# Merged value bursts, another order of maximum tiles, and divisions moved up in the tail of a fused attention and feed-forward kernel

## The chip, the cores and the metric

The kernel runs on one core of a Trainium2 chip. The metric is the device time of one execution in microseconds. The engines are PE (TensorE), DVE (VectorE), ACT (ScalarE), POOL (GpSimd) and SP (SyncE, which here issues all the DMAs).

## What is computed

The input x has 1024 tokens of 256 numbers, in float32. The reference is one block of a network:

```
x = x + layernorm(attention(layernorm(x)))
x = x + layernorm(ffn(layernorm(x)))

attention(h): gates[0] * main(h) + gates[1] * pattern(h)
  main:    16 heads with low-rank q and kv (ranks 192 and 64), 128 + 64 wide
           (the 64 with rotary positions), softmax over 1024 keys, values of 128, o_w
  pattern: 16 heads of width 16, softmax over 1024 keys, sp_o_w
ffn(h): gelu(h @ dq(up_kernel) + up_bias) @ dq(down_kernel) + down_bias
  dq: each block of 32 along K is put on an FP4 grid with a power-of-two scale
```

## The kernel before

All five engines run programs written out by hand, in order, tied by semaphores. There are three parts: a prologue (transposes, first projections), the attention, and an epilogue (output projections, normalisations, the feed-forward part).

**The attention** goes through ten slots v = 0 to 9 of 16 steps s. In slot v (1 to 8) the scores of head pair v-1 are computed while the operands of pair v are prepared. PE makes tiles, each in one of three PSUM buffers `xb` of two banks, which are used strictly in turn. A tile can start when the buffer's last tile has been read. The tiles:

- T(s): a step's pattern scores, one pair of matmuls; ACT reads them with an exponential into `ep`.
- M(s): a step's main scores, seven pairs of matmuls; ACT reads them with an exponential into `em`.
- pm (16 a slot, one pair each) and mm (16 a slot, two pairs each): scores of a quarter of the queries, of which DVE takes the maximum (lines 1170 and 1178).
- P0 to P3: projections; DVE and ACT read them (`rc` is DVE's product with the cosines). sk, sv, oT, vo: tiles of slot 0 alone, in which DVE has a share for P and sk.
- S: sums of the accumulated exponentials, which ACT reads to `sums`.

`PM_STEP` says how many pm tiles each step has; from step 3 on the first comes between T and M, a second one behind M. Then come the step's mm tile, P and S. `FIRST` is the list of slot 0's tiles. At the end of a step PE runs the value matmuls, in which four 32-column parts of the array work side by side, one set of them a `main_values` (in `pvm`) for the step before, and in odd steps a `pattern_values` (in `pvp`) as well. POOL adds up `em`, and turns the rotary halves.

DVE also quantises the feed-forward weights in between: 4 chunks of 18 steps (`quantize`), some in the slots by `QPLAN`, two a step in slot 8, and the rest behind the attention (`last_quantized`). Each pair's sums go by DMA (`gather`) to `rs`, are inverted (`main_reciprocal`, `rec_done`), and go through DRAM to a broadcast copy (`spread`). DVE then divides (`main_division`). The pattern does the same with `prs` and `prec`. All this is queued on SP in order.

**The epilogue**: PE makes eight output projections o0 to o7 (line 1539 and 1541), where o0 to o3 need the first half of the contexts and o4 to o7 also the last main division, number 15, and the last pattern division, whose result SP moves to `wst`. On DVE `mix(t)` adds the scaled parts of projection t, `first_norm(t)` and `second_norm(t)` normalise (POOL computes the root between). PE transposes the results of tiles 0 to 3 (`xT`, line 1707), projects them up (line 1770), ACT applies gelu, PE projects down, and DVE normalises and adds.

Of the kernel before, what the change touches and what calls it, by code (L numbers as in the profile page):

```python
# [33 lines left out]
P = 128  # L34
# [8 lines left out]
NP = H // 2  # L43
# [391 lines left out]
ORDER = [0, 2, 3, 1]  # L435
UNIT_STEP = {0: 0, 2: 1, 3: 3, 1: 5}
UNIT_FIRST = {0: 0, 2: 1, 3: 4, 1: 7}
PM_STEP = [0, 0, 1, 1, 1, 1, 2, 2, 1, 2, 1, 2, 2, 0, 0, 0]
MM_LATE = 9
QSTEPS = 18  # L440


QPLAN = {1: {13: 1, 14: 1, 15: 2}, 2: {0: 1, 1: 1, 13: 1, 14: 1, 15: 2}, 3: {0: 1, 1: 2, 13: 1, 14: 1, 15: 2},
# [4 lines left out]
def quantized_at(v, s):  # L448

    return (1 if s < 3 else 2) if v == NP else QPLAN.get(v, {}).get(s, 0)  # L450
# [7 lines left out]
    [("pm", 5), ("P", 3), ("pm", 6), ("sv", 2)],  # L458
    [("pm", 7), ("sk", 3), ("pm", 8)],
    [("oT", 0), ("pm", 9), ("oT", 1)],  # L460
    [("P", 1), ("pm", 10), ("oT", 2)],
    [("sk", 4), ("mm", 0), ("mm", 1)],
    [("pm", 11), ("oT", 3), ("sv", 3)],
    [("mm", 2), ("oT", 4), ("pm", 12)],
    [("mm", 3), ("oT", 5), ("pm", 13)],
    [("mm", 4), ("oT", 6), ("pm", 14)],
    [("mm", 5), ("oT", 7), ("pm", 15)],
    [("mm", 6), ("oT", 8), ("mm", 7)],
    [("vo", 0), ("vo", 1), ("mm", 8), ("vo", 2), ("vo", 3)],
]  # L470
BY_ACT = ("S", "oT", "vo", "sv")
# [8 lines left out]
def x_steps(v):  # L480
# [4 lines left out]
    for s in range(16):  # L485
        step = []
        if v <= NP:
            step.append(("T", s))
        ahead = min(PM_STEP[s], 1) if s > 2 else 0
        if v < NP:  # L490
# [3 lines left out]
        if v < NP:  # L494
            step += [("pm", pm + i) for i in range(ahead, PM_STEP[s])]
            pm += PM_STEP[s]
        late = [MM_LATE + s] if v < NP else [MM_LATE + 2 * s, MM_LATE + 2 * s + 1]
# [14 lines left out]
def attention(nc, a, d, g, sem, done):  # L512
# [11 lines left out]
    with ExitStack() as ctx:  # L524
# [44 lines left out]
        oT = ep[:, :, :].rearrange("p a b -> p (a b)").rearrange("p (h n) -> p h n", n=HID)  # L569
# [70 lines left out]
        NSTACK = 12  # L640
        QUANTIZE, SIGN = QSTEPS + 2, 15
        NBACK = 4 + 1 + 4 * PDIRECT + DIRECT
# [495 lines left out]
        def vector_program(dve):  # L1138
# [160 lines left out]
            q_step = 0  # L1299
            for v in range(NP + 1):  # L1300
                for s in range(NS):
# [9 lines left out]
                    for _ in range(quantized_at(v, s)):  # L1311
                        if q_step < 4 * QSTEPS:
                            quantize(*divmod(q_step, QSTEPS))
                            q_step += 1

            def last_quantized(part):
                for step in (range(q_step, 4 * QSTEPS - 4) if part == 0 else range(max(q_step, 4 * QSTEPS - 4), 4 * QSTEPS)):
                    quantize(*divmod(step, QSTEPS))

            return {"main_reciprocal": main_reciprocal, "main_division": main_division, "last_quantized": last_quantized,  # L1320
                    "pattern_reciprocal": pattern_reciprocal, "pattern_division": pattern_division}

        def tensor_program(pe):
# [39 lines left out]
            def main_values(it, s):  # L1363
                q, kt = s // NT, s % NT
                if kt == 0 and (it or q):

                    pe.wait_ge(ctx_out, 2 * it + q)
                pe.wait_ge(em_ready, NS * it + s + 1)
                for h in range(2):
                    for r in (0, 32):  # L1370
                        mm = pe.matmul(pvm[64 * h + r:64 * h + r + 32, :], cpair[:, kt, 0, r:r + 32], em[:, 2 * s % 8 + h, :],  # L1371
                                       start=(kt == 0), stop=(kt == NT - 1))
                mm.then_inc(pvm_done, 1)

            def pattern_values(it, kt):
                if kt == 0:
                    pe.wait_ge(vp_in[it % 2], 16 * (it // 2 + 1))
                    if it:
                        pe.wait_ge(pat_out, it)
                pe.wait_ge(ep_ready, NS * it + 2 * kt + 2)  # L1380
                for hh in range(4):
                    mm = pe.matmul(pvp[32 * hh:32 * hh + 32, :], vp[:, it % 2, kt, hh, :], ep[:, (4 * kt + hh) % 8, :],  # L1382
                                   start=(kt == 0), stop=(kt == NT - 1))
                mm.then_inc(pvp_done, 1)
# [102 lines left out]
            for v in range(NP + 1):  # L1487
                for s in range(NS):
                    for tile in xs[v][s]:
                        x_tile(v, tile)  # L1490
                    if s == 0 and v >= 2:
                        main_values(v - 2, NS - 1)
                    if s and 1 <= v <= NP:
                        main_values(v - 1, s - 1)
                    if s == 1 and v >= 2:
                        pattern_values(v - 2, NT - 1)
                    if s >= 3 and s % 2 and 1 <= v <= NP:
                        pattern_values(v - 1, (s - 3) // 2)
# [14 lines left out]

    done |= {"scores_done": (x_ready, x_index[(NP + 1, "S", 1)] + 1), "bank_emptied": bank_emptied, "ctx_back": (ctx_back, 16 * NBACK), "ctx_ready": ctx_ready, "pat_back": pat_back}
    return sync_program, pool_program, tensor_program, scalar_program, vector_program


# [28 lines left out]
def epilogue(nc, a, d, g, sem, done, out):  # L1546
# [12 lines left out]
    with ExitStack() as ctx:  # L1559
# [64 lines left out]
        def evacuated(eng, n):  # L1624

            for s, kinds in ((ev_down, ("down",)), (ev_dve, ("o", "xT"))):
                count = sum(j[0] in kinds for j in jobs[:n + 1])
                if count:
                    eng.wait_ge(s, count)
            count = sum(ups[:n + 1])  # L1630
            if count:
                eng.wait_ge(gelu_out, count)
                last = [j for j in jobs[:n + 1] if j[0] == "up" and j[1:] in hi_by_act]
                eng.wait_ge(h_hi[0], len(last))
# [179 lines left out]
        def vector_program(dve, attention_rest):  # L1814
# [8 lines left out]
            def bn_stats(tiles, srcs):  # L1823
                for t, s in zip(tiles, srcs):
                    ins = dve.bn_stats(stats[:, t, :], s)  # L1825
                link(ins)

            def bn_aggregate(kind, tiles):
                for t in tiles:
                    ins = dve.bn_aggr(mv[:, kind, t, :], stats[:, t, :])  # L1830
                ins.then_inc(var_ready, 1)
# [7 lines left out]
            def mix(t):  # L1839

                n, y = index[("o", t)], ya[:, t % 4, :]
                dve.wait_ge(ya_scaled, t + 1)
                dve.scalar_tensor_tensor(y, bank[n % 8][:, 0:HID], gates[:, t, 0:1], y, ALU.mult, ALU.add).then_inc(ev_dve, 1)
                evacuated(dve, n)
                bn_stats([t], [y])
                bn_aggregate(0, [t])

            def first_norm(t):
                y, r = ya[:, t % 4, :], res[:, t, :]
                link(normalise(0, range(t, t + 1), [y], [y]))  # L1850
                if t == 0:
                    dve.wait_ge(res_in, 16)
                dve.tensor_tensor(r, r, y, ALU.add).then_inc(ya_added, 1)
                dve.wait_ge(ya_added, t + 1)
                bn_stats([t], [r])
                bn_aggregate(1, [t])

            def second_norm(t):
                normalise(1, range(t, t + 1), [x2[:, t, :]], [res[:, t, :]]).then_inc(x2_ready, 1)
# [41 lines left out]
            attention_rest["pattern_reciprocal"](NP - 1)  # L1901
            attention_rest["last_quantized"](1)
            attention_rest["main_reciprocal"](2 * NP - 1)
            mix(0)
            first_norm(0)
            mix(1)
            second_norm(0)
            attention_rest["pattern_division"](NP - 1)
            first_norm(1)
            mix(2)  # L1910
            second_norm(1)
            attention_rest["main_division"](2 * NP - 1)
            first_norm(2)
            for t in range(3, 6):
                mix(t)
# [161 lines left out]
```

## Time and profile before

| | us |
|---|---|
| Median of 3 runs (lowest, highest) | 790.09 (786.98, 792.28) |
| The profiled execution | 788.47 |
| Its span | 786.7 |
| PE busy | 751.6 (96% of the span) |
| DVE busy | 574.2 (73%) |
| POOL busy | 431.9 (55%) |
| ACT busy | 391.9 (50%) |

Matmuls are pipelined, so a busy PE is not PE at its peak. An idle time in brackets behind a row is counted from the modelled end of the matmuls before, which is later than the moment at which the next one could have started. The starts of the matmuls are therefore the better measure of what a wait costs.

### The profile page before, as it was taken

Reading aid. Unit: us, or ns where it says so; the run is one execution under the profiler, and the core shown is the slowest. Engines: PE = TensorE matmul, PEld = TensorE weight load, DVE = VectorE, ACT = ScalarE, POOL = GpSimd, SP = SyncE. Lnnn points to the kernel's source line nnn. Section 1 sums busy time; section 2 is a strip of 40 time slices with the busy share of each in tenths; the row PEclk is TensorE's granted clock in tenths of the full one; section 3 lists DMA queues with packets and bytes.
Section 4 is the critical chain, followed back from the end, with each engine's and each line's share of the span. In section 5 each row is a group of like instructions: output and inputs, shape, how many; then the busy total and the mean of one; then the engine's idle time right before and its main releaser. Section 6 shows DMA issues by size and latency. Waiting matters only on the chain. (4 is left out here: it accounts for less than half of the span.)

```text
span 786.7 us, 13921 instructions
## 1 busy us (share of the span) xinstructions
PE 751.6 (96%) x5508; PEld 473.5 (60%) x5508; DVE 574.2 (73%) x674; ACT 391.9 (50%) x498; POOL 431.9 (55%) x281
## 2 busy tenths in 40 slices
PE   5998899999999999999999999999999999998995
PEld 5875565555555556655655565556655655457884
DVE  6886656775778577847774779577857789998647
ACT  4633455555555455555555555555555445641351
POOL 1253087437843794379437943794378445563343
PEclk9999999999999999999999999999999999998998
DMA  9897740044104430353045103530353312531001
GB/s 242 269 318 239 135 102 14 2 114 91 41 2 84 93 82 1 78 112 96 2 106 110 43 1 77 101 82 1 77 94 93 117 43 53 158 101 35 1 1 54
DMA packets 98169, 68.15 MB, mean 87 GB/s; under 512 B 66806, under 2 KB 76600, under 8 KB 97848
## 3 DMA queue, kind: packets, MB, share of 16 engines
q1 hardware_dynamic: 98104, 67.25, 34.2%
q8 instruction: 44, 0.72, 0.4%
q14 instruction: 21, 0.17, 0.1%
HBM read 41.23 MB, written 17.04 MB: 74 GB/s over the span
## 5 line engine op out<-in xcount | busy, mean ns | idle before, releaser
L1029 POOL TENSOR_TENSOR acc<-acc,em 128x1024 f32<-128x1024 f32 x96 | 234.8, 2446 | 55.0 <-ACT em L1086 52.6
L1170 DVE TENSOR_REDUCE m2p<-xb 128x2 f32<-128x1024 f32 x128 | 155.6, 1221 | 65.1 <-PE xb L1335 65.1
L1178 DVE TENSOR_REDUCE m<-xb 128x2 f32<-128x1024 f32 x128 | 155.8, 1221 | 61.9 <-PE xb L1335 61.5
L1077 ACT ACTIVATE ep<-xb 128x1024 f32<-128x1024 f32 x128 | 131.3, 1026 | 118.6 <-PE xb L1335 118.5
L1086 ACT ACTIVATE em<-xb 128x1024 f32<-128x1024 f32 x128 | 131.3, 1025 | 93.2 <-PE xb L1335 88.8
L1371 PE MATMUL pvm<-em,cpair 128*32 128x512 f32 x1024 | 136.0, 603 | 0.0
L992 POOL TENSOR_TENSOR rot<-rot,sin 128x512 f32<-128x512 f32 x32 | 41.1, 1285 | 121.1 <-DMA rot<-raw 121.1
L1335 PEld LDWEIGHTS xb<-pq,pk 49*128 49x128 f32 x256 | 23.8, 183 | 106.4 <-issue 88.8
L1029 POOL TENSOR_TENSOR acc<-em 128x1024 f32<-128x1024 f32 x16 | 38.2, 2390 | 84.1 <-PE xb L1484 75.9
L1382 PE MATMUL pvp<-ep,vp 128*32 128x512 f32 x512 | 66.6, 592 | 0.0
L1335 PE MATMUL xb<-pq,pk 49*128 49x512 f32 x256 | 64.1, 497 | 0.0
L1335 PE MATMUL xb<-kxh,qxh 64*128 64x512 f32 x256 | 55.6, 431 | 4.3 <-DVE m2p L1170 2.2
L1335 PE MATMUL xb<-qxh,kxh 64*128 64x512 f32 x256 | 52.5, 407 | 5.5 <-DVE m L1178 3.0
L1335 PE MATMUL xb<-pk,pq 48*128 48x512 f32 x256 | 54.2, 423 | 0.4 <-DVE qxl L1163 0.3
L1335 PE MATMUL xb<-mr,sel 64*128 64x512 f32 x256 | 51.0, 395 | 0.0
L1335 PE MATMUL xb<-qyh,kyl 64*128 64x512 f32 x256 | 50.7, 392 | 0.0
L1335 PE MATMUL xb<-kyh,qyh 64*128 64x512 f32 x256 | 50.6, 391 | 0.0
L1335 PE MATMUL xb<-qxl,kxh 64*128 64x512 f32 x256 | 50.6, 392 | 0.0
L1335 PE MATMUL xb<-qxh,kxl 64*128 64x512 f32 x256 | 50.4, 390 | 0.0
L1335 PE MATMUL xb<-qyh,kyh 64*128 64x512 f32 x256 | 50.1, 387 | 0.0
L1335 PE MATMUL xb<-qyl,kyh 64*128 64x512 f32 x256 | 50.1, 387 | 0.0
L1335 PEld LDWEIGHTS xb<-kxh,qxh 64*128 64x128 f32 x256 | 39.6, 305 | 13.5 <-DVE m2p L1170 4.1
(283 smaller groups left out, 1304.9 us busy)
## 6 DMA issues: line engine op xcount, KB each, us to landing
rot<-raw SPq DMA_DIRECT2D x128, 64.0 KB, 2.3
pk<-spqk_d SPq DMA_DIRECT2D x48, 128.0 KB, 4.2
sums<-rec_d SPq DMA_DIRECT2D x32, 128.0 KB, 2.9
ctx_d<-ctxr SPq DMA_DIRECT2D x14, 256.0 KB, 2.0
pq<-spqk_d SPq DMA_DIRECT2D x48, 64.0 KB, 2.3
wraw<-wst_d SPq DMA_DIRECT2D x7, 384.0 KB, 5.5
em<-in_o_w SPq DMA_DIRECT2D x1, 2048.0 KB, 7.9
vp<-vp_d SPq DMA_DIRECT2D x8, 256.0 KB, 4.7
```

What stands on the lines that cost most here:

```text
L992: pool.tensor_tensor(rot[:, n % 2, :], rot[:, n % 2, :], g["sin"][:, half_of(u % 2)], ALU.mult).then_inc(sin_done, 1)
L1029: pool.tensor_tensor(acc[:, :, :], before, em[:, j:j + 2, :], ALU.add).then_inc(added, 1)
L1077: act.activation(ep[:, j:j + 2, :], src[:, :, :], ACT.Exp, scale=PAT_SCALE).then_inc(ep_ready, 1)
L1086: act.activation(em[:, j:j + 2, :], src[:, :, :], ACT.Exp, scale=MAIN_SCALE).then_inc(em_ready, 1)
L1170: dve.tensor_reduce(m2p[:, 2 * tp:2 * tp + 2, t, kt], src[:, :, :], AX, ALU.max).then_inc(x_dve, 1)
L1178: dve.tensor_reduce(m2[:, q, :, t, kt], src[:, :, :], AX, ALU.max).then_inc(x_dve, 1)
L1335: mm = pe.matmul(out[:, h, :], w[at, :], x[at, :], start=(n == 0), stop=(n == len(pairs) - 1))
L1371: mm = pe.matmul(pvm[64 * h + r:64 * h + r + 32, :], cpair[:, kt, 0, r:r + 32], em[:, 2 * s % 8 + h, :], start=(kt == 0), stop=(kt == NT - 1))
L1382: mm = pe.matmul(pvp[32 * hh:32 * hh + 32, :], vp[:, it % 2, kt, hh, :], ep[:, (4 * kt + hh) % 8, :], start=(kt == 0), stop=(kt == NT - 1))
```

## The change

It has four parts. `PM_STEP` gets another spread: steps 4, 8 and 10 have two pm tiles instead of one, steps 6, 9 and 11 one instead of two. `together` names steps whose `main_values` are not run in their own step but in the next one, ahead of that one's: steps 2 and 14 of slots 1 to 7, steps 4, 6, 10, 12 and 14 of slot 8. In slot 0 two tiles change places in steps 7 and 8, and two in step 14. At the end, DVE's last reciprocals stand between quantisation steps, two steps earlier than before, the last pattern division ahead of `mix(0)`, and the last main division ahead of `first_norm(1)`.

```diff
-PM_STEP = [0, 0, 1, 1, 1, 1, 2, 2, 1, 2, 1, 2, 2, 0, 0, 0]
+PM_STEP = [0, 0, 1, 1, 2, 1, 1, 2, 2, 1, 2, 1, 2, 0, 0, 0]
...
+def together(v, s):
+
+    return s in ((4, 6, 10, 12, 14) if v == NP else (2, 14))
...
-    [("P", 1), ("pm", 10), ("oT", 2)],
-    [("sk", 4), ("mm", 0), ("mm", 1)],
+    [("P", 1), ("sk", 4), ("oT", 2)],
+    [("pm", 10), ("mm", 0), ("mm", 1)],
...
-    [("mm", 6), ("oT", 8), ("mm", 7)],
+    [("oT", 8), ("mm", 6), ("mm", 7)],
...
-                for step in (range(q_step, 4 * QSTEPS - 4) if part == 0 else range(max(q_step, 4 * QSTEPS - 4), 4 * QSTEPS)):
+                ends = [q_step] + [max(q_step, 4 * QSTEPS - n) for n in (6, 2, 0)]
+                for step in range(ends[part], ends[part + 1]):
...
-                    if s and 1 <= v <= NP:
+                    if s and 1 <= v <= NP and not together(v, s):
+                        if together(v, s - 1):
+                            main_values(v - 1, s - 2)
                         main_values(v - 1, s - 1)
...
             attention_rest["pattern_reciprocal"](NP - 1)
             attention_rest["last_quantized"](1)
             attention_rest["main_reciprocal"](2 * NP - 1)
+            attention_rest["last_quantized"](2)
+            attention_rest["pattern_division"](NP - 1)
             mix(0)
             first_norm(0)
             mix(1)
             second_norm(0)
-            attention_rest["pattern_division"](NP - 1)
+            attention_rest["main_division"](2 * NP - 1)
             first_norm(1)
             mix(2)
             second_norm(1)
-            attention_rest["main_division"](2 * NP - 1)
             first_norm(2)
```

## Rows read from the trace of the kernel before

**Rows 1.** Timeline of PE, slot 3, around a burst: start, length, line, operands, count.
```profile
306.35 0.40 PE L1335 MATMUL xb<-kxh,qxh 64*128 64x512 f32 x2
306.58 0.40 PE L1335 MATMUL xb<-kyh,qyh 64*128 64x512 f32 x2
306.91 1.06 PE L1371 MATMUL pvm<-em,cpair 128*32 128x512 f32 x8
307.79 1.04 PE L1382 MATMUL pvp<-ep,vp 128*32 128x512 f32 x8
308.76 0.50 PE L1335 MATMUL xb<-pq,pk 49*128 49x512 f32 x2
309.10 0.39 PE L1335 MATMUL xb<-pk,pq 48*128 48x512 f32 x2
```

**Rows 2.** Timelines of DVE and PE, slot 4, steps 2 and 3.
```profile
340.05 1.23 DVE L1170 TENSOR_REDUCE m2p<-xb 128x2 f32<-128x1024 f32 x1 [3.63 <-PE xb L1335]
341.19 1.22 DVE L1178 TENSOR_REDUCE m<-xb 128x2 f32<-128x1024 f32 x1
...
342.46 0.50 PE L1335 MATMUL xb<-qxh,kxh 64*128 64x512 f32 x2 [0.32 <-DVE m L1178]
```

**Rows 3.** Timeline of PE, slot 4, M4.
```profile
349.34 0.50 PE L1335 MATMUL xb<-qxh,kxh 64*128 64x512 f32 x2 [0.38 <-DVE rc L1154]
```

**Rows 4.** Timelines of ACT and PE, slot 3, step 14.
```profile
319.30 1.02 ACT L1086 ACTIVATE em<-xb 128x1024 f32<-128x1024 f32 x1 [0.59 <-PE xb L1335]
...
319.66 1.06 PE L1371 MATMUL pvm<-em,cpair 128*32 128x512 f32 x8
```

**Rows 5.** Timelines of DVE and PE, slot 1 and then slot 4, steps 6 and 7.
```profile
126.53 1.22 DVE L1178 TENSOR_REDUCE m<-xb 128x2 f32<-128x1024 f32 x1
...
127.08 0.40 PE L1335 MATMUL xb<-pk,pq 48*128 48x512 f32 x2
127.81 0.50 PE L1335 MATMUL xb<-qxh,kxh 64*128 64x512 f32 x2 [0.32 <-DVE m L1178]
...
361.71 0.39 PE L1335 MATMUL xb<-pk,pq 48*128 48x512 f32 x2
362.48 0.62 PE L1335 MATMUL xb<-kxh,qxh 64*128 64x512 f32 x2 [0.38 <-DVE m2p L1170]
```

**Rows 6.** Timelines of ACT and PE, slot 8, step 1, the sums tile.
```profile
645.70 1.02 ACT L1086 ACTIVATE em<-xb 128x1024 f32<-128x1024 f32 x1 [1.20 <-PE xb L1335]
...
646.77 1.06 PE L1484 MATMUL xb<-acc,ones 128*32 128x512 f32 x8 [0.18 <-ACT em L1086]
```

**Rows 7.** Timeline of PE, slot 0, step 8: the sk tile.
```profile
66.49 0.50 PE L1327 MATMUL xb<-xh,kxl 128*128 128x512 f32 x1 [1.54 <-DVE qyl L1151]
```

**Rows 8.** Timeline of DVE, the end: quantisation, reciprocal, two divisions, mix(4).
```profile
712.28 1.25 DVE L1293 STREAM_TRANSPOSE qm0l_f<-qm0h_f 128x1024 f32<-128x1024 f32 x1
...
714.17 0.20 DVE L1188 RECIPROCAL rs<-rs 128x8 f32<-128x8 f32 x1
...
719.39 0.69 DVE L1207 TENSOR_TENSOR prec<-pvr,prec 128x512 f32<-128x512 f32 x1
...
723.41 0.68 DVE L1198 TENSOR_TENSOR work_f<-ctxr,sums 128x512 f32<-128x512 f32 x1
...
732.29 0.48 DVE L1843 SCALAR_TENSOR_TENSOR ya<-c_bank,gates,ya 128x256 f32<-128x256 f32 x1 [2.46 <-ACT ya L1791]
```

**Rows 9.** DMA issues, 695 to 787 us: count, KB each, us to landing.
```profile
sums<-rec_d SPq DMA_DIRECT2D x2, 128.0 KB, 2.9
```

**Rows 10.** Timeline of PE, the end: o4, o5 and the transposes begin.
```profile
724.20 1.19 PE L1539 MATMUL c_bank<-rot,kxh 128*128 128x256 f32 x2 [3.36 <-DVE work_f L1198]
...
731.59 0.59 PE L1539 MATMUL c_bank<-rot,kxh 128*128 128x256 f32 x2
...
735.90 1.04 PE L1707 MATMUL c_bank<-ident,x 128*128 128x128 f32 x8
```

**Rows 11.** Busy time by microsecond; the granted PE clock stands behind POOL's.
```profile
723.00:724.00 1.00, 0.00 (x0) 0.00 (x0) 1.00 (x3) 0.00 (x0) 0.74 (x3) 0.72 0.21 37
```

## The prediction

> **What bounds the kernel now.** I read the page first (TensorE, PE, is busy for 96% of the span), then PE's timeline slot by slot, then those of DVE and ACT where PE waits. In slots 1 to 8 PE issues almost without a gap: a full-speed pair of matmuls every 0.23 us. The reader should see two things in [rows 1]. The four-column matmuls of the values run in bursts, 0.88 us for one set. Around a burst PE loses a little: the last pair before it lasts 0.33 instead of 0.23 us, the last set 0.97 instead of 0.88, and the first pair behind it 0.34 instead of 0.23. So one switch into a burst and out again costs 0.10 + 0.09 + 0.11 = 0.30 us. That is what the change of the values can save: it makes one burst of two. Outside the bursts a tile can only start when its PSUM buffer is empty. There are three buffers in turn, so the fourth tile waits for the first. PE's few waits in a slot are of that kind [rows 2, 3]. At the end it is DVE that PE waits for.
>
> **Values of step 1 put behind those' successors, slots 1 to 7 (steps 2 and 3).** Without the burst in step 2, T3 and the next pm come sooner, but M3 cannot: its buffer is that of the mm tile of step 2, and DVE reduces the pm tile first (from 340.05) and that one second (from 341.19, 1.22 us, so to 342.41). M3 starts at 342.46 with the burst in place, directly behind this reduction [rows 2]. It starts at the same time without it. So the burst filled a time in which PE would have idled, and the set, now issued in step 3, adds its 0.87 us there. Who takes part of that back: in slots 2 to 6 the next M waits anyway for DVE's rc, until 349.34 [rows 3]; T4 would come at 349.10, its pm 0.34 later and M at 349.68, and it no longer pays the 0.11 of a restart. Loss 0.34 - 0.11, some 0.24 us. Slots 1 and 7 have no such wait, and lose the whole 0.87. Sum 5 x 0.24 + 2 x 0.87 = 2.9 us.
>
> **Values of step 13 put into step 15's burst.** The tiles are T14, M14, mm, T15, M15, so M15 takes M14's buffer. ACT empties that from 319.30 for 1.02 us, to 320.32, and PE could use it at about 320.37. PE is done with mm at 319.66 - 0.09 = 319.57 [rows 4] and with T15 at 319.80. It idles 0.57 us and pays a restart of 0.10; it saves 0.30. Loss 0.37 us, seven times: 2.6 us. In slot 8 there are no mm tiles behind step 3, M takes T's buffer and not M's, and merging does save 0.30 us in steps 4, 6, 12 and 14; in step 10 the sums tile stays a burst of its own, so nothing is saved. That is 1.2 us of PE, and it buys nothing: at the end PE stands idle for 3.4 us waiting for DVE (below), and DVE's work of slot 8 does not follow PE.
>
> **The pm tiles.** Steps 4, 8 and 10 get two instead of one, steps 6, 9 and 11 one instead of two. Even steps have one set of values, odd ones two. With two pm tiles and an mm tile DVE has 3 x 1.14 = 3.4 us of reductions (the step between those of [rows 2]), and M of the next step takes the buffer of the mm tile, which is reduced last. The trace has this case: slot 1, step 6 to 7. The mm tile is reduced from 126.53 for 1.22 us, M starts at 127.81; without a wait it would start 0.24 behind the pm pair of 127.08, at 127.32. With the restart that costs 0.59 us [rows 5]. So steps 4 to 5 and 8 to 9 get 0.59 us each. Step 6 loses its wait: 0.59 us in slot 1; in slots 2 to 7 the wait for m2p, where 361.71 to 362.48 should have been 0.24, and the pair behind it is longer too: 0.76 us. In step 10 the sums tile is the fifth: before, it took the pm tile's buffer; now it takes M10's. A sums tile behind M shows the price: in slot 8 ACT starts M's exponentials at 645.70, for 1.02 us, and the sums tile starts at 646.77 [rows 6], which is 1.28 us behind the end of M. In step 10 only pm, mm and the switch (0.24 + 0.47 + 0.09) lie between: wait 0.48 us. Slots 2 to 7: 0.59 - 0.76 + 0.59 + 0.48 = 0.90; slot 1: 1.07. Sum 6.5 us. Step 12 is as before.
>
> Of this the Trainium skill states both sides. By TensorEngine Tiling (Array Packing), Key Properties, a change of tiling mode drains TensorE; the trace agrees with its 0.30 us, and by that rule alone the values' part of the sum would be a gain, rival A's. The same page, PSUM Bottleneck, says that tiling speeds up TensorE and not the evacuation of PSUM; that is the rule which speaks against merging, and the buffer waits above agree with it: by it the sum is the forecast's.
>
> **Slot 0.** The sk tile before pm no longer takes the buffer of P1: PE's wait of 1.54 us on qyl [rows 7] goes. Behind it pm now waits for qyl and pm 11 for the reduction of pm 10, and DVE's reductions of mm follow one by one; by their order they come 1.15 us sooner. Of the exchange of oT and mm at the end I count nothing, since M0 waits there for the rows that a DMA brings. Gain 1.15 us, bounds 0 and 1.5.
>
> **The end.** DVE runs without a gap from before the last reciprocals on. The main one now stands in front of the last two quantisation steps, that is where the transpose of 712.28 starts, and not at 714.17 [rows 8]. Its answer goes through a small store and a broadcast that lands 2.9 us after its issue [rows 9]; allowing as much again for the store and the issue it is there by 718.1. The main division itself stands where the pattern's stood, at 719.39, plus 0.6 us for that one, which now comes ahead of mix(0): 720.0 instead of 723.41 [rows 8]. So it finds its operand. The pattern division waits for its own broadcast, and mix(0) and all of DVE's epilogue are queued behind it; its reciprocal is 1.9 us earlier as well, and if the answer were late, each tenth would cost a tenth. On SP the pattern's move is queued behind the main broadcast, which is 1.9 us earlier too, so that it ends before 720. PE's fifth projection, o4, which began at 724.20 behind the division [rows 10], can start at 720.8. What comes before it on PE ends 1.2 us earlier than now, so the idle time shrinks from 3.4 to 1.2 us. With the 3.4 us the granted clock fell in the microsecond 723 to 724, after 2.6 us of idleness, to the lower of its two levels, 1.2 GHz [rows 11], and o4 took 7.39 us, o5 behind it 4.31 [rows 10]. After the idle 1.54 us of [rows 7] it had stayed at 2.4 GHz. So o4 ends at 725.1 instead of 731.6. What is next late is DVE: mix(4), which waited 2.46 us before 732.29 [rows 8] for that projection, now follows its predecessor, at 730.1, and the transposes that need its result come at 731.7 instead of 735.90 [rows 10]. From there to the end PE is the chain. Gain 4.2 us. Bounds: 1.1, if the new idle time of 2.2 us before the transposes lets the clock fall (the lower clock cost 7.39 - 4.31 = 3.1), and 5, if DVE also loses small waits for POOL's roots.
>
> **Sum.** 2.9 + 2.6 + 6.5 - 1.15 - 4.2 = +6.6 us. The profiled execution took 788.47 us, 1.8 more than its span; it becomes 795.1. The median of the three runs is 1.6 above it, 790.09, and there I put the forecast: 796.7 us, 0.8% slower. One per cent, 7.9 us, is about what a measurement of this kernel can tell from no change.
>
> **Rivals.** A, the evacuation keeps up, so that merging pays (18 switches of 0.30, 5.4 us), the pm tiles cost nothing, and the end and slot 0 gain as above: 790.1 - 5.4 - 5.4 = 779.3. For it: the switch is real. Against it: each wait above follows from a duration and from the order of three buffers. It needs reductions under 0.7 us. 0.12. B, as forecast, but the clock falls in the new idle time before the transposes: + 3.1, so 799.8. For it: 2.2 us is near the 2.6 after which it fell; against: it stayed up after 1.54. 0.15. C, the pm tiles change places and nothing else: the wait goes from step 6 to step 5, and in steps 8 to 10 DVE and ACT are early enough, so 6.5 becomes 0: 790.2. For it: no wait stands in steps 8 to 12 now. 0.2. D, DVE, later in each slot, delays its quantisation and the rows of maxima that the next slot needs, 1 us a slot more: 803.7. Decides if a wait on DMA mr shows up. 0.03. The forecast itself: 0.5.
>
> **Range and chances.** The forecast's own terms can be off by 0.3 us a slot and by the bounds of the end, so 792 to 801; C and B draw it to 789 and 802, which leaves out A, D and little else. Under 782.2: A alone, 0.12. Over 798: B, D and a fifth of the forecast, 0.28. Between: 0.60.
>
> **What would show it.** Right: in slots 1 to 7 new idle times of PE in front of M5 and M9 released by DVE m, in front of the sums tile and of M15 released by ACT em, none before mm 15; a slot about 80 instead of 78.7 us; four merged bursts in slot 8; PE idle about 1.2 us before o4 at full clock, transposes 4.2 us earlier against the last reciprocal. Wrong: a slot not longer than 78.7 us would mean that my order of buffers or the durations do not hold; a clock at 1.2 GHz behind the idle times of the end takes most of its gain.

## The result, and the profile after

| | before | after |
|---|---|---|
| Median of the runs beside each other (lowest, highest) | 789.45 (786.98, 792.28), 6 runs | 797.17 (795.11, 800.19), 6 runs |
| Profiled execution, its span | 788.47, 786.7 | 800.19, 798.4 |

The ratio is 1.0099, with a 95% interval of 1.0067 to 1.0131: 5.3 to 10.3 us slower. The forecast was 796.7 us, 6.6 us slower. Of all the runs behind this document one stands apart, with 1439.75 us, in the kernel with M3 ahead of the pm tile below; nothing on record explains it, and the ratio there leaves it out.

The page of the changed kernel, busy times by engine. PE has the same work, 0.7 us more of it; its share falls since the span grows.

```profile
PE 752.3 (94%) x5508; PEld 476.1 (60%) x5508; DVE 575.3 (72%) x674; ACT 390.3 (49%) x498; POOL 434.2 (54%) x281
```

The profiled execution was the slowest of its six, and its span is 11.7 us longer than that of before, more than the medians differ. So I cut both spans at the same instructions before comparing anything:

| stretch | before | after | difference | forecast |
|---|---|---|---|---|
| start to P0 of slot 1 | 93.67 | 96.83 | +3.16 | -1.15 |
| to the sums tile of slot 8 | 553.10 | 564.76 | +11.66 | +12.0 |
| to DVE's last group of four multiply-adds | 57.22 | 57.38 | +0.16 | 0 |
| to the end | 82.71 | 79.43 | -3.28 | -4.2 |

The instructions at which I cut: first DVE's multiply-adds of the kernel before (its P0 stands at 93.67, its sums tile is in [rows 6]), then P0, the sums tile and the multiply-adds of the changed kernel.

```profile
703.99 5.00 DVE L1280 SCALAR_TENSOR_TENSOR qm0h_f<-qm0l_f,qm0h_f 128x1024 f32<-128x1024 f32 x4
...
96.83 0.62 PE L1422 MATMUL xb<-qm,wst 64*128 64x512 f32 x1
661.59 1.07 PE L1490 MATMUL xb<-acc,ones 128*32 128x512 f32 x8 [0.19 <-ACT em L1091]
718.97 5.00 DVE L1285 SCALAR_TENSOR_TENSOR qm0h_f<-qm0l_f,qm0h_f 128x1024 f32<-128x1024 f32 x4
```

How far one profile speaks for the second line can be seen from the kernels of the experiments below. Three others leave slots 1 to 7 as before; their profiles give 553.80, 553.11 and 553.97 us. Two others have these slots as the changed kernel has them, and give 562.97 and 563.75. In the mean the slots cost 10.3 us (563.8 against 553.5). The 11.66 of this pair, so close to the forecast's 12.0, is in part luck.

The first line is no cost that the change can be charged with. Of its 3.16 us, 1.18 stand ahead of P0 of slot 0 (38.85 us against 37.67), where the two kernels are the same. Busy times by stretch, slot 0 of the changed kernel (behind POOL's the granted clock): it was at the lower level in two places, where the profile of before shows 1.00 throughout. At 0.83 over 10 us, 1.7 us are lost each time.

```profile
60.00:70.00 10.00, 8.30 (x32) 5.67 (x31) 4.90 (x6) 3.89 (x7) 3.84 (x3) 0.83 0.96 350
90.00:100.00 10.00, 8.33 (x48) 5.66 (x46) 2.00 (x2) 3.50 (x5) 0.00 (x0) 0.83 0.78 177
```

**The slots.** Timeline of PE, slot 4 of the changed kernel: step 3 (T3, M3), step 5 (pm, M5), step 9 (pm, M9), step 10 (mm, sums tile), step 15 (T15, M15).

```profile
350.10 0.49 PE L1341 MATMUL xb<-pq,pk 49*128 49x512 f32 x2 [0.41 <-ACT em L1091]
351.67 0.50 PE L1341 MATMUL xb<-qxh,kxh 64*128 64x512 f32 x2 [0.51 <-DVE m L1183]
...
362.63 0.40 PE L1341 MATMUL xb<-pk,pq 48*128 48x512 f32 x2
363.34 0.50 PE L1341 MATMUL xb<-qxh,kxh 64*128 64x512 f32 x2 [0.32 <-DVE m L1183]
...
382.70 0.40 PE L1341 MATMUL xb<-pk,pq 48*128 48x512 f32 x2
383.42 0.50 PE L1341 MATMUL xb<-qxh,kxh 64*128 64x512 f32 x2 [0.32 <-DVE m L1183]
...
390.24 0.40 PE L1341 MATMUL xb<-kyh,qyh 64*128 64x512 f32 x2
391.05 0.64 PE L1490 MATMUL xb<-acc,ones 128*32 128x512 f32 x4 [0.41 <-ACT em L1091]
...
408.31 0.39 PE L1341 MATMUL xb<-pq,pk 49*128 49x512 f32 x2
409.12 0.50 PE L1341 MATMUL xb<-qxh,kxh 64*128 64x512 f32 x2 [0.42 <-ACT em L1091]
```

Read the starts. M5 begins 0.71 us behind its pm tile, where 0.24 would do, and its first pair takes 0.10 more: 0.57 us, as M7 of slot 1 did before [rows 5]. M9 shows the same, 0.58. The sums tile begins 0.81 behind mm's last pair, where a burst needs 0.33: 0.48 us. M15 begins 0.81 behind T15: 0.57 too many. The waits of the old kernel at mm 15 [rows 5] and, in this slot, at M4 [rows 3] are gone. A wait in front of T3 for ACT is new, but costs nothing, since M3 behind it waits for DVE anyway.

A wait that I had not reckoned with stands in slot 3. Timelines of ACT and PE of the changed kernel: the exponential of T3 stands on ACT behind the conversion of the rotated query, which waits for POOL, and mm of step 3 needs T3's buffer. The wait itself is not new. The kernel before has it too, in slot 3 alone, with 1.03 us; that is the row put first.

```profile
265.55 0.62 PE L1335 MATMUL xb<-kxh,qxh 64*128 64x512 f32 x2 [1.03 <-ACT ep L1077]
...
271.70 0.63 ACT L1109 ACTIVATE qxh<-rc 128x512 fp32r<-128x512 f32 x1 [3.58 <-POOL rc L1004]
272.23 1.01 ACT L1082 ACTIVATE ep<-xb 128x1024 f32<-128x1024 f32 x1
...
273.29 0.62 PE L1341 MATMUL xb<-kxh,qxh 64*128 64x512 f32 x2 [1.64 <-ACT ep L1082]
```

In slot 8 the bursts of step 4, 6, 12 and 14 are merged. Timeline of PE: sixteen matmuls in one burst, and another wait that I had not seen, of the values of step 8.

```profile
691.66 0.64 PE L1377 MATMUL pvm<-em,cpair 128*32 128x512 f32 x4 [0.58 <-ACT ctxr L1128]
...
705.23 1.92 PE L1377 MATMUL pvm<-em,cpair 128*32 128x512 f32 x16
```

**The end.** Timelines of DVE and PE of the changed kernel, beside [rows 8, 10], and two microseconds of the busy times, beside [rows 11].

```profile
727.61 0.20 DVE L1193 RECIPROCAL rs<-rs 128x8 f32<-128x8 f32 x1 [0.39 <-DMA rs<-sums]
730.11 0.69 DVE L1212 TENSOR_TENSOR prec<-pvr,prec 128x512 f32<-128x512 f32 x1 [0.46 <-DMA prec<-prec_d]
735.88 0.68 DVE L1203 TENSOR_TENSOR work_f<-ctxr,sums 128x512 f32<-128x512 f32 x1
745.96 0.45 DVE L1851 SCALAR_TENSOR_TENSOR ya<-c_bank,gates,ya 128x256 f32<-128x256 f32 x1
...
736.66 0.67 PE L1547 MATMUL c_bank<-rot,kxh 128*128 128x256 f32 x2 [1.67 <-DVE work_f L1203]
741.06 0.59 PE L1547 MATMUL c_bank<-rot,kxh 128*128 128x256 f32 x2
747.60 0.63 PE L1715 MATMUL c_bank<-ident,x 128*128 128x128 f32 x4 [2.06 <-DVE x L1844]
...
736.00:737.00 1.00, 0.34 (x2) 0.34 (x3) 0.56 (x1) 0.00 (x0) 0.91 (x2) 1.00 0.07 1
746.00:747.00 1.00, 0.00 (x0) 0.00 (x0) 0.93 (x4) 0.05 (x1) 0.79 (x2) 1.00 0.00 0
```

PE's idle time before o4 is 1.67 us instead of 3.36, o4 takes 4.40 us instead of 7.39, and mix(4) waits for nothing. Before the transposes PE now idles 2.06 us, and in this execution the clock stayed at 2.4 GHz through both. But DVE has two new waits, 0.39 us for the gathered sums and 0.46 for the pattern's broadcast.

### The profile page after: what moved, and what is told of

Same layout as the page of the kernel before. It is cut to its first block and busy times, and to the rows that moved or that the text cites. A ratio compares the mean times of both kernels' runs of the same rounds, so it can differ in the third digit from the quotient of the medians.

```text
span 798.4 us, 13921 instructions
## 1 busy us (share of the span) xinstructions
PE 752.3 (94%) x5508; PEld 476.1 (60%) x5508; DVE 575.3 (72%) x674; ACT 390.3 (49%) x498; POOL 434.2 (54%) x281
## 5 line engine op out<-in xcount | busy, mean ns | idle before, releaser
L1377 PE MATMUL pvm<-em,cpair 128*32 128x512 f32 x1024 | 132.1, 601 | 0.6 <-ACT ctxr L1128 0.6
L1341 PE MATMUL xb<-kxh,qxh 64*128 64x512 f32 x256 | 53.9, 418 | 2.6 <-ACT ep L1082 1.6
L1377 PEld LDWEIGHTS pvm<-em,cpair 128*32 128x32 f32 x1024 | 23.6, 108 | 47.5 <-issue 46.4
```

Of the source, the lines that this page charges most:

```text
L1341: mm = pe.matmul(out[:, h, :], w[at, :], x[at, :], start=(n == 0), stop=(n == len(pairs) - 1))
```

## The experiments

Four kernels undo one part of the changed kernel, eight do one part, or two, on the kernel before. Where a part is given in microseconds without more words, it is the ratio's distance from 1, times the time of the kernel before; the difference of the two medians can lie up to 1.6 us from it. Besides the ratio I read the same stretches as above. The kernels of one group ran on one chip and share the runs of the kernel before.

### One part of the changed kernel undone

Beside 787.88 us for the kernel before (10 runs). By its ratio, the changed kernel would take 795.7 there.

**Values together in slot 8 alone.**

```diff
-    return s in ((4, 6, 10, 12, 14) if v == NP else (2, 14))
+    return s in ((4, 6, 10, 12, 14) if v == NP else ())
```

> The changed kernel with the value bursts of slots 1 to 7 as before (merges in slot 8 only). Buffer theory: the merges of steps 2 and 14 cost more in waits of PE than their switches save, 0.24 + 0.37 us in slots 2 to 6, so this is 4 to 5.5 us faster than the changed kernel (about 792.5 us, 0.4% above the kernel before), a slot lasts 0.6 us less than 79.9, and PE's waits in front of T3 and M15 on ACT em are gone while those of M5, M9 and the sums tile stay. Rival, merging pays (each merged burst saves 0.30 us) and the loss is the pm tiles' alone: 4 us slower than the changed kernel.

793.0 us, ratio 1.0067 (1.0051 to 1.0084). The stretch over slots 1 to 7 is 558.50 us, 4.5 to 6.3 less than in the three profiles that have the slots of the changed kernel. By the ratios the difference is some 2.5 us, and their intervals overlap. So it is the stretch that says that merging there costs and doesn't pay.

**The old spread of the pm tiles.**

```diff
-PM_STEP = [0, 0, 1, 1, 2, 1, 1, 2, 2, 1, 2, 1, 2, 0, 0, 0]
+PM_STEP = [0, 0, 1, 1, 1, 1, 2, 2, 1, 2, 1, 2, 2, 0, 0, 0]
```

> The changed kernel with the pm tiles spread as before. Buffer theory: the waits of 0.59 us in front of M5 and M9 and 0.48 us at the sums tile go, the one at mm 15 in step 6 comes back, 6 to 6.5 us faster than the changed kernel (about 791 us), a slot lasts 0.9 us less. Rival, pm tiles only change places: no difference.

791.4 us, ratio 1.0048 (1.0033 to 1.0064): about 4 us back. The stretch over the slots is 556.55 us, 6.4 to 8.2 less than in those three profiles. Both readings put the spread above the merged bursts as the largest loss, the ratios (1.0048 and 1.0067) with intervals that overlap.

**The old order of the end.** `last_quantized` in two parts and the two divisions back in their places.

> The changed kernel with the order of the end as before. Theory: the fifth projection starts 3.4 us later behind the last main division, PE idles over 4 us in front of it (1.2 us more than before, since slot 8's merges end PE's slot sooner), the clock falls to 1.2 GHz for it, and the kernel is 3 to 4.2 us slower than the changed one (about 801 us). Rival, the end is bound by DVE's chain of normalisations, and the division's place gives nothing: no difference.

798.61 us, ratio 1.014 (1.0122 to 1.0159): some 3 us slower than with the new order. Its stretch at the end is 82.2 us where the changed kernel has 79.4. The end is the part that pays.

**The old list of slot 0.** The three lines of `FIRST` back.

> The changed kernel with slot 0's tile list as before. Theory: PE's wait of 1.5 us on qyl comes back, tiles behind it 1.15 us later, so up to 1.2 us slower (798.3 us). Rival, what ends slot 0 is SP's queue and its loads in front of the rows of maxima, so that M0 of slot 1 starts at the same distance from the end of the prologue: no difference.

798.0 us, ratio 1.0132 (1.0112 to 1.0152). Its interval touches the changed kernel's. It speaks for a gain by the new list, but of a size that the next group doesn't confirm.

### One part on the kernel before: the values

Beside 789.09 us (35 runs).

**Values of step 1 in step 3, slots 1 to 7.** The new `together`, with

```diff
+    return s in (() if v == NP else (2,))
```

> The kernel before, with one part of the change: in slots 1 to 7 the values of step 1 are issued in step 3, behind those of step 2. My theory: the burst of step 2 stood in a time in which PE would wait for the reduction of the mm tile, so a wait of some 0.5 us for DVE's m appears in front of M3, M3 starts when it started before, and the set adds 0.87 us behind it, 0.24 us of it left in slots 2 to 6 and all of it in slots 1 and 7: 2.9 us slower, ratio 1.0037. Rival A (the evacuation keeps up): 7 switches of 0.30 us fewer, 2.1 us faster, 0.997. A third reading, from the slots of the changed kernel: the late set also pushes the next step's M behind rc in every slot, 7 x 0.87 = 6 us slower, 1.0077.

791.49 us, ratio 1.0037 (1.0021 to 1.0054), as forecast. Timeline of PE, slot 4 of this kernel, step 3:

```profile
341.37 0.51 PE L1340 MATMUL xb<-pq,pk 49*128 49x512 f32 x2 [0.41 <-ACT em L1091]
341.82 0.62 PE L1340 MATMUL xb<-pk,pq 48*128 48x512 f32 x2
342.95 0.50 PE L1340 MATMUL xb<-qxh,kxh 64*128 64x512 f32 x2 [0.51 <-DVE m L1183]
...
345.01 0.63 PE L1340 MATMUL xb<-kxh,qxh 64*128 64x512 f32 x2 [0.17 <-ACT ep L1082]
```

M3 starts 15.01 us behind P0 of its slot (327.94), and so it did before (342.46, P0 at 327.45). The time in step 2 that the burst filled is now idle. In slots 1 and 7 the way from P0 to P1 grows by 0.93 and 0.88 us, one set; in slots 2 to 6 by 0.04 to 1.18, 0.48 in the mean where I had 0.24. No M4 waits for `rc` there any more. In slots 3, 4 and 6 PE waits at mm of step 3 instead, for the exponential of T3 (1.03, 0.17 and 0.92 us), and this wait stands ahead of the moved set, so that it can't cover it.

**Values of step 13 in step 15, slots 1 to 7.** The same with `(14,)`.

> The kernel before, with one part of the change: in slots 1 to 7 the values of step 13 are issued in step 15. My theory: M15 waits some 0.5 us for ACT to empty the buffer of M14, less the switch saved: 7 x 0.37 = 2.6 us slower, ratio 1.0033. Rival A: 2.1 us faster, 0.997. No difference (0 us, 1.000) would mean that something later in PE's order, such as the projections at the start of the next slot, takes the wait back.

788.0 us, ratio 0.9986 (0.9974 to 0.9998). The forecast's 2.6 us aren't there. The wait is. Timelines of PE, SP and DVE of this kernel, slot 3 to 4:

```profile
319.30 0.39 PE L1340 MATMUL xb<-pq,pk 49*128 49x512 f32 x2
320.11 0.51 PE L1340 MATMUL xb<-qxh,kxh 64*128 64x512 f32 x2 [0.42 <-ACT em L1091]
...
326.44 0.33 SPq L972 DMA_DIRECT2D ctx_d<-ctxr  x1
...
324.69 1.73 DVE L1203 TENSOR_TENSOR ctxr<-ctxr,sums 128x512 f32<-128x512 f32 x1
```

The same instructions of the kernel before:

```profile
326.88 0.33 SPq L967 DMA_DIRECT2D ctx_d<-ctxr  x1
...
324.93 1.92 DVE L1198 TENSOR_TENSOR ctxr<-ctxr,sums 128x512 f32<-128x512 f32 x1
```

The way from P1 to the next P0 grows by 0.30 to 0.37 us in each of slots 1 to 6, as my sum had it (0.37). But from P0 to P1 slots 2 to 5 are 0.35, 0.49, 0.37 and 0.98 us shorter than before, slot 6 0.40 longer, and the whole stretch over the slots is 553.03 against 553.10. The last kernel below has the same slots and gives 554.03; the mean of these two is that of the four profiles with the slots of before, 553.5. Behind slot 7 the way from P1 to the sums tile of slot 8 is even 0.36 shorter: M1 of slot 8, which waited 0.43 us for DVE's `m` before, doesn't wait any more. What sets the time from P0 to P1 in these slots is SP. It issues, one behind the other, the context's store as soon as DVE has divided, then 5.5 us of operand loads, then the rows for the rotation; POOL turns them, and DVE's `rc`, for which M4 waits [rows 3], and ACT's conversion hang on POOL. DVE's division, and with it SP's store, don't wait for M15: the store comes 1.11 us ahead of P0 in this kernel, 0.57 ahead of it before. So PE gets back in slot 4 what it has lost in slot 3, and M4 of slot 4 waits no more.

**The same as in step 2, with M3 ahead of the pm tile of step 3.**

```diff
-        ahead = min(PM_STEP[s], 1) if s > 2 else 0
+        ahead = min(PM_STEP[s], 1) if s > 3 else 0
```

> As the one with the values of step 1 in step 3, but step 3 runs T3, M3, pm, where it was T3, pm, M3. Then M3 takes the buffer of step 2's pm tile, which DVE reduces first (1.2 us sooner), and pm the one of the mm tile. If the order of the three buffers is what made merging in step 2 lose, the wait in front of M3 goes, and the pair of kernels differs: here at most 1.2 us slower than the kernel before (5 x 0.24, the slots whose M4 waits for rc), ratio 1.0015, against 1.0037. If the loss comes from the set's own length behind M3, it stays at 1.0037. A rival: the mm tile of step 3 now takes T3's buffer, and waits for ACT's exponentials of T3, up to 1 us a slot: 1.005 and more.

792.9 us, ratio 1.0046 (1.003 to 1.0063). The interval holds both the 1.0037 of the set's own length and the 1.005 of the rival, so the ratio doesn't tell them apart; the waits at mm, in each of slots 2 to 6, are the rival's. Timelines of PE and ACT, slot 4 of this kernel:

```profile
342.75 0.51 PE L1340 MATMUL xb<-pq,pk 49*128 49x512 f32 x2 [0.41 <-ACT em L1091]
343.19 0.51 PE L1340 MATMUL xb<-qxh,kxh 64*128 64x512 f32 x2
...
346.39 0.62 PE L1340 MATMUL xb<-kxh,qxh 64*128 64x512 f32 x2 [1.07 <-ACT ep L1082]
...
344.80 0.63 ACT L1109 ACTIVATE qxh<-rc 128x512 fp32r<-128x512 f32 x1 [2.10 <-POOL rc L1004]
345.33 1.00 ACT L1082 ACTIVATE ep<-xb 128x1024 f32<-128x1024 f32 x1
```

M3's wait is gone, so it was the order of the buffers that made it. In slots 1 and 7 the way from P0 to P1 grows by 0.45 and 0.58 us now, where it was 0.93 and 0.88. In slots 2 to 6 the wait comes back at mm (0.34 to 1.82 us), behind the same chain from SP over POOL to ACT, and nothing is won.

### One part on the kernel before: pm tiles, end, slot 0

The end with the merged bursts of slot 8 ran with the kernels on the values above (beside 789.09 us, 35 runs), the others beside 789.07 us (31 runs).

**The new spread of the pm tiles alone.**

> The kernel before with the other order of the pm tiles alone. My theory (waits for DVE's m in front of M5 and M9, for ACT's em in front of the sums tile, none for m2p in front of mm 15): 6.5 us slower, ratio 1.0083; less, some 4.5 us or 1.0057, if in slots 3, 4 and 6 the waits that hang on SP's queue (mm 12 for POOL's rope, M4 for rc) hide a part, as the slots of the kernel with no values together in slots 1 to 7 suggest. Rival C (the tiles only change places): 0 us, 1.000.

796.47 us, ratio 1.0074 (1.0044 to 1.0103): 5.8 us, while the medians lie 7.4 apart. The stretch over slots 1 to 7 grows by 8.16 us. Timeline of PE, slot 4, M4 and M5:

```profile
354.69 0.51 PE L1340 MATMUL xb<-qxh,kxh 64*128 64x512 f32 x2 [0.37 <-DVE rc L1159]
...
358.57 0.40 PE L1340 MATMUL xb<-pk,pq 48*128 48x512 f32 x2
359.29 0.51 PE L1340 MATMUL xb<-qxh,kxh 64*128 64x512 f32 x2 [0.32 <-DVE m L1183]
```

The new waits stand at M5, M9 and the sums tile of each slot, the one at mm 15 is gone: rival C is out. In the slots in which M4 doesn't wait before (1 and 7) P0 to P1 grows by 0.86 and 0.94 us, the pm pair of step 4 and M5's wait. From P1 to the next P0, where a pm pair less, the wait of mm 15 and those of M9 and the sums tile meet, it is 0.02 to 0.06 (0.26 in slot 1). That makes 0.9 to 1.0 a slot, where the forecast has 0.90, and 1.12 in slot 1 (1.07). In slots 2 to 6 it comes to 1.21 in the mean: M4 waited for `rc` here too, and started later behind P0 than before (22.71 against 21.89 us in slot 4). It is the same chain, this time against me.

**The new order of the end, with the merged bursts of slot 8 (4, 6, 12, 14).**

> The kernel before with two parts of the change: the order of the end (last quantisation steps, pattern division ahead of mix 0, main division ahead of the second first norm), and the merged bursts of slot 8 (steps 4, 6, 12 and 14; that of step 10 left out, since the sums tile makes a burst of its own there). My theory: the end gains 3.3 to 4.2 us, as it did between the kernels before and after, and the merging in slot 8 nothing, since PE waits for DVE at the end: 3.7 us faster, ratio 0.9953. If merging in slot 8 does pay, another 1.2 us: 0.994. If the clock falls in the 2.1 us of idleness before the transposes: 0.6 us faster at most, 0.999.

787.74 us, ratio 0.9984 (0.997 to 0.9998).

**The new order of the end alone.**

> The kernel before with the order of the end alone. By the trace of the one with the order of the end and the merged bursts of slot 8, the stretch from the last four multiply-adds of the quantisation to the end is 3.4 us shorter, while its median was only 1.3 us below. My theory: merging in slot 8 buys and costs nothing, so this one is the same as that one, ratio 0.9984, and its own end 3.4 us shorter. Rival: merging in slot 8 costs some 2 us (values of step 8 wait for ACT's ctxr), then 0.996.

787.79 us, ratio 0.9986 (0.9971 to 1.0001). Nothing tells these two apart. The traces say the same more sharply. With the merged bursts the output projections begin 54.57 us behind the sums tile instead of 55.33, although PE waits 0.45 us for `ctxr` in between; but o4 begins 17.60 us behind DVE's four multiply-adds instead of 17.54. So merging in slot 8 saved PE time and bought nothing. But 1.1 or 1.3 us are less than the 3.3 that the stretch at the end had shown. Timeline of PE, o4 and the transposes, and the busy times, of the kernel with the end alone; behind the fence, what they mean.

```profile
723.14 0.67 PE L1547 MATMUL c_bank<-rot,kxh 128*128 128x256 f32 x2 [0.70 <-issue]
...
734.06 1.23 PE L1715 MATMUL c_bank<-ident,x 128*128 128x128 f32 x8 [2.05 <-DVE x L1844]
...
735.00:736.00 1.00, 1.00 (x5) 0.82 (x4) 0.93 (x3) 0.92 (x2) 0.00 (x0) 0.50 0.06 16
```

Behind the idle 2.05 us the clock was at 1.2 GHz here, and it was not in the profile of the kernel above it, with the same 2.05 us. I read the stretch from the four multiply-adds to the end in all fourteen profiles. The last 6 us are left out of the second column, since the clock falls there in every one of them.

| order of the end | lost to the clock (1 less the granted clock, times the time), us | stretch, us | profiles |
|---|---|---|---|
| old | 3.4 | 82.2 to 82.7 | 5 |
| old | 1.7 | 81.1, 81.4 | 2 |
| new | 0 | 79.3 to 79.4 | 4 |
| new | 1.7 | 80.9 to 81.0 | 3 |

So the new order is worth some 3.3 us where the clock stays up behind it (and the old one pays its 3.4), and in the mean of the profiles 2.1 us (82.1 against 80.0). The ratios, 1.1 and 1.3 us here and 3 in the changed kernel, with intervals of some 1.1 to each side or more, lie on both sides of that.

**The new list of slot 0 alone.**

> The kernel before with the list of slot 0 alone (sk 4 before pm 10, oT 8 before mm 6). My forecast was 1.15 us faster, 0.9985; by the traces of the changed kernel the wait for qyl only moves, with a new wait of P1 for ACT's ep (0.3 to 0.8 us) ahead of it: 0 to 0.5 us slower, 1.000 to 1.0006. If the stretches at the lower clock in slot 0, which every profile of a kernel with this list showed and those of before did not, belong to it, 1.5 to 4 us slower, 1.002 to 1.005.

789.53 us, ratio 0.9995 (0.9979 to 1.0011): no difference that can be told. Timelines of PE and ACT, slot 0 of this kernel:

```profile
61.41 0.50 PE L1421 MATMUL xb<-qm,wst 64*128 64x512 f32 x1 [0.61 <-ACT ep L1096]
66.65 0.62 PE L1340 MATMUL xb<-pk,pq 48*128 48x512 f32 x2 [0.89 <-DVE qyl L1156]
...
60.76 1.08 ACT L1096 ACTIVATE ep<-xb 128x512 f32<-128x512 f32 x2 [2.53 <-DMA wst_d<-wall]
```

The wait for `qyl` is 0.89 instead of 1.54 us [rows 7], and pm 11 follows P1 1.11 us sooner (its first pair at 68.59 behind 61.41, before at 69.57 behind 61.28). But P1 itself waited 0.61 us, since ACT stood at a store until 60.76. M0 of slot 1, at the far end, waits for its rows from a DMA in seven of the fourteen profiles, with 0.57 to 1.05 us. From P0 of slot 0 to P0 of slot 1 it takes 55.3 to 58.3 us in the five profiles with this list (56.9 in the mean) and 55.4 to 57.6 in the nine with the old one (56.4). And the granted clock fell in slot 0 in all five profiles of kernels with this list, with 1.7, 3.4 or 6.8 us lost (1 less the granted clock, times the time, from 60 to 100 us); with the old list in four of nine, with 1.7 us. Whether the list has a part in that, nothing here settles.

**The end and the values of step 13 together**, the two parts that measured below 1, on the kernel before.

> A version that may beat both: the kernel before with the order of the end, and the values of step 13 in step 15's burst in slots 1 to 7. If their gains add (1.3 and 1.1 us), 2.4 us faster, 0.997; if the second is only chance, 0.9984 as with the end alone.

788.02 us, ratio 0.998 (0.9964 to 0.9995), 1.6 us faster (1.0 by the medians): the lowest ratio of all, but not apart from those of the two kernels with the new end, whose medians are lower.

## Why the prediction was right, and where it was not

**What bounds the slots.** Right. Every wait that I named stands where the three buffers in turn put it, within 0.03 us of its price: M5 and M9 0.57 and 0.58 (0.59), the sums tile 0.48 (0.48), M15 0.57. That is the reason why the sign was right. The size of the three terms together, 12.0 us, is another matter. The changed kernel's trace has 11.66, the mean of the profiles 10.3, and the traces of the parts alone have 8.2, 4.1 and -0.1 where I had 6.5, 2.9 and 2.6. That their sum comes out near is luck. A slot (2 to 6) lasts 79.9 to 81.9 us instead of 78.5 to 79.8.

**Values of step 1.** Right in place and in slots 1 and 7; the ratio of the part alone gives 2.9 us, as forecast, its trace 4.1. In the 0.24 us of slots 2 to 6 the cover was to be M4's wait for `rc`, and I took the chain behind it as fixed. With the set moved no M4 waits for `rc`: where the chain is late, PE waits one tile earlier, at mm, and pays for the set behind that. The mean was 0.48 us. Among the four profiles with the slots of before, the way from P0 to P1 of one such slot differs by 0.4 to 0.9 us, so the single slots say little.

**Values of step 13: the step that failed.** "Loss 0.37 us, seven times: 2.6 us." The loss is there, some 0.3 us in each slot. That it adds up to the end is wrong: alone, the part measured 1.1 us below the kernel before (0.2 to 2.1). I had used M4's wait as cover for the set of step 1, and didn't ask what the same wait does with a delay from the slot before. It covers that as well, since SP's chain starts from DVE's division and not from PE's last tile. That the SP chain is the cause is read off the rows; no run moved it alone. For slot 7 the rows show another cover, M1's wait in slot 8.

**The pm tiles.** Right in mechanism, and in size where nothing else waits: 0.9 to 1.0 us a slot, 1.12 in slot 1. By the ratio 5.8 us (6.5 forecast), by the medians 7.4, by the trace 8.2; what the trace has beyond the forecast lies nearly all in slots 2 to 6, where the chain of `rc` and `ep` comes in. The rule of the Trainium skill that I set against merging (TensorEngine Tiling (Array Packing), PSUM Bottleneck: tiling speeds up TensorE and not the evacuation) agrees with these traces in step 2: M3 starts 15.01 us behind P0 with the burst and without it, when DVE has emptied the buffer. With the drain that the same page states under Key Properties, which would have made merging pay (rival A), the trace agrees as well, by the 0.30 us lost around a burst. That was worth nothing wherever PE had to wait for a buffer or a later engine anyway. Rival C went with the waits at M5, M9 and the sums tile, and rival D with the time: no wait of PE for DMA `mr` stands in slots 2 to 8.

**Slot 0.** Gain 1.15 us: the local one is there, 1.11 us. Over the kernel it is not found: 0.4 us by the ratio, with zero inside the interval, and 0.5 the other way by the medians. A store that holds ACT and the rows that a DMA brings to M0 stand around it, and I counted the end of slot 0 at nothing for that reason but not its middle.

**The end.** Mechanism right, size too large: 4.2 us forecast, 3.28 in the changed kernel's trace. Of the difference, 0.46 is the pattern division's wait for its broadcast, which I had in time, and 0.39 a wait of DVE for the gathered sums. Rival B, the clock in the new idle time, was put as a case of its own with 3.1 us and a chance of 0.15. It came true in three of seven profiles, with 1.6 us each, and not in that of the changed kernel. That merging in slot 8 buys nothing holds.

**The sum.** 6.6 us forecast, 7.7 by the medians. The misses offset each other: step 13's values were 3.7 us too dear, slot 0 and the end together 1.6 to 3.7 us too good, the rest is in the chain that I took as fixed. So the total is right in part by luck, and says less for the sum than its terms do. The parts measured alone add up to 5.8 + 2.9 - 1.1 - 1.3 - 0.4 = 5.9 us by their ratios and to 7.8 by the medians, both inside the interval of the whole.

## What to carry to other kernels

Merging short bursts of another tiling saves a real switch, but a burst that stands where the next tile waits for its buffer is free, and moving it away makes it cost its full length. Price each moved piece by the start of the next instruction that is pinned by another engine, and ask of each pin what it hangs on: a delay ahead of a pin that doesn't follow PE is given back, one behind it is not. Where one profile is compared with one profile, cut both spans at the same instructions and look at the granted clock of each stretch before any difference is put down to an edit. And read the same stretch in every other profile that shares its code: here that moved 11.7 us to 10.3.

## What was not expected of the hardware

The granted clock isn't a function of the idle time alone. Behind 2.05 or 2.06 us without a matmul before the transposes it fell in three profiles and stayed at 2.4 GHz in four, and behind 3.36 to 4.17 us before o4 it fell in seven of seven, but with two different losses. In slot 0, where PE's waits from 60 us on are 1.7 us at most, it fell in nine of fourteen profiles, between 61.9 and 94.4 us, as in these two microseconds of the kernel with the new end and the merged bursts of slot 8 (busy times, the clock behind POOL's), with PE busy throughout:

```profile
73.00:74.00 1.00, 1.00 (x6) 1.00 (x6) 0.11 (x1) 0.00 (x0) 0.06 (x1) 0.50 0.00 0
74.00:75.00 1.00, 1.00 (x7) 0.78 (x6) 0.00 (x0) 0.11 (x1) 0.00 (x0) 0.50 0.00 0
```

One such stretch costs 1.6 to 1.7 us, as much as most edits here are worth. The runs of the kernel before, 31 of one program on one chip, span 7 us (786.45 to 793.47).
